# Third layer: neighbouring key tiles scored together, with 32-row shift products side by side

## The reference

```python
Q = (x @ Wq.T).reshape(b, n, H, R)
K = (x @ Wk.T).reshape(b, n, H, R)
V = (x @ Wv.T).reshape(b, n, H, d)
attn = jnp.einsum('bnhr,bmhr->bhnm', Q, K)
attn = jax.nn.softmax(attn, axis=-1)
out = jnp.einsum('bhnm,bmhd->bnd', attn, V)
```

## Time and profile before

| What | Value |
|---|---|
| Median of 3 runs | 1762.69 us (1760.91 to 1763.16) |
| The profiled execution's own time | 1757.49 us |
| Its span, first to last instruction | 1755.6 us |
| PE busy | 1668.1 us, 95% of the span |
| PEld busy | 1004.2 us, 57% |
| DVE busy | 996.3 us, 57% |
| ACT busy | 837.4 us, 48% |
| POOL busy | 406.9 us, 23% |

### The profile page before, as it was taken

How to read it: one execution, slowest core, us unless ns; L and a number is a source line. 1 busy time by engine, 2 the same in 40 slices (tenths; PEclk the granted TensorE clock), 3 DMA queues, 4 the chain that set the end, 5 groups by cost and what they waited for, 6 DMA issues and landing times. The chain is left out here.

```text
span 1755.6 us, 22810 instructions
## 1 busy us (share of the span) xinstructions
PE 1668.1 (95%) x8686; PEld 1004.2 (57%) x8686; DVE 996.3 (57%) x1649; ACT 837.4 (48%) x1048; POOL 406.9 (23%) x331
## 2 busy tenths in 40 slices
PE   7799999999889999999999999999999997999997
PEld 4232222223555667878778786877778673444443
DVE  4555555543675454444555454454555447888886
ACT  5667777776435533333334343343344343444442
POOL 1000000000553322030211112030211205655563
PEclk8799999999889999999999999999999998999999
DMA  2222222222007610000000000000000001000000
GB/s 81 52 49 49 49 49 49 49 49 111 17 26 190 150 27 1 2 0 2 1 1 1 1 1 1 1 1 1 1 1 1 1 1 51 7 7 7 6 13 12
DMA packets 20553, 49.10 MB, mean 28 GB/s; under 512 B 1184, under 2 KB 2080, under 8 KB 19680
## 3 DMA queue, kind: packets, MB, share of 16 engines
q1 hardware_dynamic: 20448, 47.66, 11.1%
HBM read 45.17 MB, written 2.36 MB: 27 GB/s over the span
## 5 line engine op out<-in xcount | busy, mean ns | idle before, releaser
L524 ACT ACTIVATE probs<-ps 128x1024 f32<-128x1024 f32 x256 | 245.9, 1024 | 88.7 <-PE ps L780 85.8
L1972 PEld LDWEIGHTS ps_o<-v,probs 128*128 128x128 f32 x2048 | 236.8, 192 | 35.2 <-issue 30.1
L1972 PE MATMUL ps_o<-v,probs 128*128 128x129 f32 x2048 | 248.2, 278 | 1.7 <-ACT probs L1656 1.2
L1656 ACT ACTIVATE probs<-ps_ring 128x1024 f32<-128x1024 f32 x128 | 127.0, 1023 | 201.9 <-PE ps_ring L1953 201.6
L1748 DVE TENSOR_REDUCE negmax<-ps_o 128x2 f32<-128x1024 f32 x64 | 78.5, 1226 | 137.0 <-PE ps_o L1928 137.0
L794 PE MATMUL ps<-probs,v 128*32 128x512 f32 x1024 | 136.7, 607 | 0.9 <-DVE o_sb L601 0.9
L1649 ACT ACTIVATE xn<-ps_ring,pack 128x512 f32<-128x512 f32 x64 | 40.6, 685 | 164.0 <-PE ps_ring L1493 164.0
L2174 POOL TENSOR_TENSOR rs<-r,state 128x512 f32<-128x512 f32 x64 | 86.2, 1349 | 91.6 <-DVE state L2340 91.6
L1761 DVE RECIPROCAL rden<-ps_o 128x2 f32<-128x2 f32 x128 | 21.5, 168 | 147.8 <-PE ps_o L1972 147.8
L2340 DVE TENSOR_TENSOR_SCAN state<-decay,state,kv 128x511 f32<-128x511 f32 x64 | 99.1, 1548 | 6.9 <-issue 1.5
L780 PEld LDWEIGHTS ps<-q_stack,k_stack 32*128 32x128 f32 x512 | 31.4, 185 | 123.3 <-issue 96.1
(11 more groups left out here) (418 smaller groups left out, 3431.3 us busy)
## 6 DMA issues: line engine op xcount, KB each, us to landing
cwb<-combine_by_expert SPq DMA_DIRECT2D x8, 2048.0 KB
score<-score_by_expert SPq DMA_DIRECT2D x15, 1024.0 KB, 8.0
pack<-pack_dram SPq DMA_DIRECT2D x1, 3840.0 KB, 15.2
x<-x_in SPq DMA_DIRECT2D x2, 1024.0 KB, 6.1
out<-x SPq DMA_DIRECT2D x8, 256.0 KB, 2.0
pack<-pack_dram SPq DMA_DIRECT2D x1, 1992.0 KB, 8.1
pack<-pack_dram SPq DMA_DIRECT2D x1, 1543.0 KB, 6.4
pack<-pack_dram SPq DMA_DIRECT2D x1, 1140.0 KB, 9.4
```

The lines of the kernel that those rows point to most:

```text
L524: nc.scalar.activation(probs[n % 3][:, 2 * half:2 * half + 2, :], ps, ACT.Exp, scale=float(HD0) ** -0.5).then_inc(read, 1)
L1656: nc.scalar.activation(probs[:, n % 2, m, :, :], ps, ACT.Exp).then_inc(read, 1)
L1972: last = nc.tensor.matmul(ps_o[:, i, k * (D + 1):(k + 1) * (D + 1)], probs[:, (b * PAIRS + p) % 2, m, j, queries], v[:, m, h, :], start=(m ...
```

## The change

The four shift products of two neighbouring key tiles (two heads, two tiles) become 32 rows deep and are issued one behind the other, each in its own 32 rows. For that the shift row of each head is copied to two rows: head 0 to rows 0 and 32, head 1 to rows 64 and 96; each of the two transfers now writes two rows. The new `scores_of_two` issues the six part products of tile m, then those of tile m + 1, then the four shift products; tile m is reported done after the first two of these, tile m + 1 after the last two.

It takes the place of two calls of `scores` in six places of each batch: tiles (0, 0) and (0, 1), tiles (0, 2) and (0, 3), the last two tiles of head pairs 1 and 2, and both halves of head pair 3. In head pair 3 the second tile moves ahead of a call of `times_v`. The first two tiles of head pairs 1 and 2 still go through `scores`, whose shift products are now 32 rows deep too.

```diff
-                for j in range(2):
-                    sp.dma_start(sh_row[n % 2][64 * j:64 * j + 1, :].rearrange("o (m t) -> o m t", t=P),
-                                 rows[NBLK * j:NBLK * j + NBLK, n % 2, :]).then_inc(sh_loaded[n % 2], 16)
+                for a in range(2):
+                    sp.dma_start(sh_row[n % 2][32 * a:P:64, :].rearrange("j (m t) -> j m t", t=P), rows[:, n % 2, :]
+                                 ).then_inc(sh_loaded[n % 2], 16)
...
+            def shift_product(ps, n, j, a):
+                group = slice(64 * j + 32 * a, 64 * j + 32 * a + 32)
+                return nc.tensor.matmul(ps[:, j, :], single(ones_row[group, :]), single(sh_row[n % 2][group, :]), start=False, stop=True)
+
+            def scores(b, p, m):
+                if m == 0:
+                    shift_rows_loaded(b, p)
+                ps, done = empty(pe, ("score", b, p, m))
+                score_products(ps, p, m)
                 for j in range(2):
-                    last = nc.tensor.matmul(ps[:, j, :], single(ones_row[head_rows(j), :]), single(sh_row[n % 2][head_rows(j), :]),
-                                            start=False, stop=True)
+                    last = shift_product(ps, b * PAIRS + p, j, 0)
                 last.then_inc(done, 1)
+
+            def scores_of_two(b, p, m):
+                if m == 0:
+                    shift_rows_loaded(b, p)
+                two = []
+                for a in range(2):
+                    two.append(empty(pe, ("score", b, p, m + a)))
+                    score_products(two[a][0], p, m + a)
+                for a, (ps, done) in enumerate(two):
+                    for j in range(2):
+                        last = shift_product(ps, b * PAIRS + p, j, a)
+                    last.then_inc(done, 1)
...
-                scores(b, 0, 0)
-                scores(b, 0, 1)
+                scores_of_two(b, 0, 0)
                 down(b, lambda: maxima(b, 1, 3))
-                scores(b, 0, 2)
-                scores(b, 0, 3)
+                scores_of_two(b, 0, 2)
                 turn_max(b, 1)
...
                         times_v(b, p, s)
-                        if p + 1 < PAIRS and s < 3:
-                            scores(b, p + 1, s)
-                            if s == 2:
-                                scores(b, p + 1, 3)
-                                if p + 2 < PAIRS:
-                                    turn_max(b, p + 2)
+                        if p + 1 < PAIRS and s < 2:
+                            if p + 2 < PAIRS:
+                                scores(b, p + 1, s)
+                            elif s == 0:
+                                scores_of_two(b, p + 1, 0)
+                        if p + 1 < PAIRS and s == 2:
+                            scores_of_two(b, p + 1, 2)
+                            if p + 2 < PAIRS:
+                                turn_max(b, p + 2)
```

More of the change, by code:

```diff
@@ L1940, in turn_max, with shift_rows_loaded, score_products @@
                                     ident).then_inc(done, 1)
-            def scores(b, p, m):
+            def shift_rows_loaded(b, p):
                 n = b * PAIRS + p
-                if m == 0:
-                    pe.wait_ge(sh_loaded[n % 2], 32 * (n // 2 + 1))
-                ps, done = empty(pe, ("score", b, p, m))
+                pe.wait_ge(sh_loaded[n % 2], 32 * (n // 2 + 1))
+            def score_products(ps, p, m):
                 keys = slice(m * P, (m + 1) * P)
```

## The result

The changed kernel took 1787.44 us (median of 5 runs, 1785.61 to 1791.08) against 1760.91 us (1756.17 to 1763.16): 1.0158 times as long, 95% interval 1.0135 to 1.0181. The forecast was 1792 us with a range from 1774 to 1800. The profiled executions have spans of 1783.7 and 1755.6 us, 28.1 us apart.

What follows compares the result with a forecast made beforehand. TensorE's own instruction stream was taken to bound the third layer. 3.71 us per batch times 7 is 26.0, plus 3.13 in the last batch: +29 us on 1762.7, so 1792 us, range 1774 to 1800.

Steps and rivals of the forecast that it cites:

- (0,2),(0,3) before the mean: First tile's exponential starts 0.90 us later, and the mean waits for it: +0.90 us per batch.
- singles (1,0),(1,1): Unjoined tiles: one change into 32 rows and one back, 0.42 us each tile, 0.84 us for both.
- (1,2),(1,3): Next V product needs all four exponentials and starts at 1003.71 in place of 1003.44: +0.27 us per batch.
- (3,0),(3,1): Two changes of depth and one group go, one change to 32 rows comes: -0.41 us per batch.
- (3,2),(3,3): Second V product starts at 1029.86 in place of 1029.49, behind later exponentials: +0.37 us per batch.
- The price of a change of depth: TensorE switching between 64 and 32 rows: 0.10 us before the first group and 0.11 in it, 0.21 together.
- The half price: Rival, 12%: a 64/32 change drains but weights load ahead, 0.10 in place of 0.21; +18 us, 1781 us.
- the free change: Rival, 7%: 64 and 32 rows mix freely, only waits and small terms remain; +7 us, 1770 us.
- The waits: Mean and variance have no slack behind the exponential, so its 0.90 us delay counts in full at each.
- The faster rival: Rival, 5%: packing pays at the six quads, 1.77 us saved per batch or 14 us, 1748 us.
- The quad in two groups: Rival, 6%: four products run as two pairs, 0.23 us more in each of six places; +11 us, 1803 us.
- The last batch: Its own sum, 0.90 + 0.42 + 0.90 + 0.42 + 0.90 - 0.41: 3.13 us.

Runs made afterwards that it cites:

- the singles alone: Changed kernel with the shift products of the four single tiles per batch back at 64 rows, joined pairs left as they are: 1781.3 us, 1.0118 times the kernel before.
- depth everywhere: Kernel before with every shift pair 32 rows deep from one copy of the shift row, nothing joined: 1792.52 us, 1.0181 times the kernel before.
- both causes removed: Changed kernel with the singles' shift products at 64 rows and shift products first in joined pairs, six quads left in: 1762.66 us, 1.0008 times the kernel before.

## Why the prediction was right, step by step

| Step, per batch | Forecast us | Measured us (batch 3) |
|---|---|---|
| (0,0),(0,1) before the down projection | 0 | 0.01 |
| (0,2),(0,3) before the mean | 0.90 | 0.88 |
| singles (1,0),(1,1) | 0.84 | 0.83 |
| (1,2),(1,3) | 0.27 | 0.53 |
| singles (2,0),(2,1) | 0.84 | 0.80 |
| (2,2),(2,3) before the variance | 0.90 | 0.90 |
| (3,0),(3,1) | -0.41 | -0.42 |
| (3,2),(3,3) | 0.37 | 0.53 |

The measured numbers are differences of the distance between the same two starts in both traces; the two joined pairs (1,2),(1,3), for instance, stand 11.40 us later after than before at their first product (1010.91 to 999.51), and the tile behind them 11.92 later (1017.24 to 1005.32), which is 0.53 before rounding.

- **The price of a change of depth** was the choice on which most hung: 64 beside 32 rows stood in no row of before. The 0.21 us held: 0.32, 0.43 and 0.34 us between starts, 1.55 us per batch for the singles alone, 4.43 for depth everywhere. The half price and the free change, rivals with 12% and 7%, are out. The reason given for the part inside the first group holds as well: the quad's weights are loaded when its products start, not ahead (998.15).
- **The waits** held: the start times of the earlier trace rows had shown no slack, and moving the shift products ahead gave back 2.38 us per batch. The faster rival fell with this: the quad does take one group's time, but with both causes removed the places with nothing but a quad agree with the kernel before within 0.01 us, so the six of them gain nothing.
- **The quad in two groups** is out: four products in 0.51 us.
- **Two terms were too small.** I took 0.06 us from the end of an exponential to the V product, read at the mean. The V product starts 0.25 us after (1015.04 to 1015.29). The two places lose 0.53 each, 0.42 more per batch together than forecast, and 2 x 0.19 of it is this distance. The other terms were 0.1 too large in sum.
- **The last batch** cost 4.6 us and not 3.1: tile (0,0) of it starts 25.64 us later than before (1405.65 to 1380.01), the mean behind head pair 3's last tiles 30.24 later (1468.18 to 1437.94). The missing 1.5 us is the clock after the 2.15 us wait, a term that the forecast did not have; it priced that wait by its length alone.
- **The whole time** came so near in part by luck. The layer grew by 7 x 4.02 + 4.6 = 32.7 us, 3.7 more than the 29 forecast, while the span grew by 28.1: in these two executions the rest of the program, which the change does not touch, was 4.6 us shorter after the change. Of that, 2.4 us lie ahead of the layer's first mean (it comes 1.5 us earlier, though its batch was 0.9 longer up to there) and 2.2 behind the last of the means that follow, where it is 309.6 us to the end in place of 311.8. There the granted clock (the first of the last three numbers) differs, before and after:

```profile
1443.80:1755.60 311.80, 282.34 (x806) 138.80 (x804) 254.56 (x284) 129.53 (x184) 168.67 (x127) 0.96 0.04 14
```

```profile
1474.10:1783.70 309.60, 279.27 (x806) 137.79 (x804) 254.48 (x284) 129.52 (x184) 168.64 (x127) 0.98 0.04 15
```

Whole times go with this clock: of 29 runs of the kernel before, the six with a mean of 0.966 to 0.968 took 1763.1 to 1766.7 us, the four with 0.975 or 0.976 took 1754.2 to 1757.7, and the five runs of the changed kernel read 0.974 to 0.976. What lowers it in one run and not in another is not shown, and the 2.4 us ahead of the layer stay open (the clock up to 655 us is 0.95 in both). So the forecast stands 4.6 us above the median although the layer's growth was put 3.7 us too small: the runs that it started from were 1.8 us above this comparison's, and the rest is the shorter rest of the program.

## What to carry to other kernels

Packing small products side by side saves a group's time (0.23 us here), but each switch between row depths costs about as much (0.21); at the end of every tile nothing is left of it. Whether it pays where products of one depth stand in a row, no run here tried. Before work of two tiles is joined, look up what is released by the first: here an exponential of 1 us stood with no slack in front of the next step, although the trace showed hardly any idle time. Where whole times scatter more than the effect, the period of a repeated row in the trace can separate what the runs don't; here it repeated within 0.1 us of 104.

## What the runs showed that was not expected

After a wait of 2.15 us in an otherwise dense stream the granted clock read 0.71 over 5 us, and 0.95 over the next 5, so for part of them TensorE ran at its lower level (1.2 GHz), and the wait cost 1.5 us beyond its length. It fell the same way in the three other runs with waits of 1.92 to 2.14 us at this place, and stayed at 1.00 in all runs with waits of 1.23 to 1.46.

The distance from an exponential's end to TensorE's start was 0.05 us at the mean and 0.25 us at a V product. At the V product the trace shows two semaphore instructions one after the other in TensorE's queue in between (L1563 at 1015.1 and L1989 at 1015.2 us), at the mean none that ends before it starts; that these are the 0.2 us was not tested.
